# Softplus as one ScalarE function, routing by replaced maxima, and new orders for all engines

## The reference, cut to what matters

```
# state-space block, per sequence
delta = softplus(ts @ dt_w + dt_b)                  # 256 tokens x 256 channels
A = -exp(A_log)                                     # 256 channels x 16 states
dA = exp(A * delta);  new = dA * state + delta * B * h
y = sum over states of (new * C) + D * h;  y * silu(gate), then @ out_w
# feed-forward
probs = softmax(x @ router_w)                       # 8 experts
top_vals, top_idx = top_k(probs, 2);  weights = top_vals / sum(top_vals)
out = sum over e of weight_e * ((x @ w_up[e]) * silu(x @ w_gate[e])) @ w_down[e]
```

## Time and profile before

| | |
|---|---|
| runs | 628.21 us median of 3 (626.58 to 628.58) |
| profiled execution | span 623.0 us (from the first to the last instruction; no other time of it is on record) |
| TensorE busy | 592.8 us, 95% |
| VectorE busy | 499.4 us, 80% |
| ScalarE busy | 400.5 us, 64% |
| GpSimd busy | 392.6 us, 63% |
| mean granted clock of TensorE | 0.989 of 2.4 GHz |

### The profile page before, as it was taken

The page is one execution under the profiler, slowest core; times in us unless marked ns, Lnnn a source line. Parts: engine busy times, 40 slices in busy tenths (PEclk is TensorE's granted clock), DMA queues, the critical chain, the costliest instruction groups (busy, mean ns, idle before and its releaser), DMA issues.

```text
span 623.0 us, 13130 instructions
## 1 busy us (share of the span) xinstructions
PE 592.8 (95%) x4502; PEld 546.7 (88%) x4502; DVE 499.4 (80%) x1094; ACT 400.5 (64%) x897; POOL 392.6 (63%) x368
## 2 busy tenths in 40 slices
PE   6778999699999999999999999999999999999997
PEld 5434786398989999999999999999999999999997
DVE  6798778886998799988998899889988896454454
ACT  7977727766768775878587867776576643516240
POOL 1486564589686987788787978697867773001000
PEclk9779999999999999999999999999999999999999
DMA  7952204130030403021302203030303000000000
GB/s 280 275 169 110 82 2 147 59 119 34 9 140 16 142 4 149 11 89 62 127 23 90 71 12 138 23 136 3 149 12 146 1 15 12 12 2 14 2 22 10
DMA packets 18468, 45.45 MB, mean 73 GB/s; under 512 B 2847, under 2 KB 13664, under 8 KB 14178
## 3 DMA queue, kind: packets, MB, share of 16 engines
q1 hardware_dynamic: 18402, 44.61, 20.1%
HBM read 40.15 MB, written 1.31 MB: 67 GB/s over the span
## 4 chain that ended last, share of the span: by engine, by line
PE 75%; POOL 6%; DVE 5%; issue 3%; ACT 2%; DVEq 0%; POOLq 0%; ACTq 0%
PE ps L1327 25%; PE ps L1131 13%; PE ps L1132 12%; PE ps L1133 12%; PE ps L1376 2%; POOL st L530 2%; DVE st L1005 2%; POOL yacc L543 2%; PE ps L1223 1%; PE ps L1388 1%; PE ps L1295 1%; DVE ps L991 1%; PE ps L1126 1%; PE ps L1367 1%; PE ps L1266 1%
## 5 line engine op out<-in xcount | busy, mean ns | idle before, releaser
L530 POOL TENSOR_TENSOR st<-st,rows_ring 128x512 f32<-128x512 f32 x128 | 165.7, 1298 | 58.5 <-DVE st L1005 58.2
L1327 PE MATMUL ps<-down,inner_ring 128*128 128x128 f32 (+1 forms) x1408 | 171.5, 274 | 0.0
L1327 PEld LDWEIGHTS ps<-down,inner_ring 128*128 128x128 f32 (+1 forms) x1408 | 165.5, 191 | 1.7 <-issue 1.0
L787 ACT ACTIVATE sg<-ps 128x512 f32<-128x512 f32 x176 | 104.3, 596 | 88.1 <-PE ps L1133 76.9
L1080 DVE TENSOR_TENSOR inner_ring<-sg,ps 128x512 f32<-128x512 f32 x176 | 118.7, 678 | 48.6 <-PE ps L1133 25.2
L1005 DVE TENSOR_TENSOR_SCAN st<-dA,ps 128x512 f32<-128x512 f32 x128 | 154.6, 1211 | 2.8 <-ACT dA L730 1.6
L543 POOL TENSOR_TENSOR yacc<-yacc,st 128x512 f32<-128x512 f32 x96 | 123.8, 1289 | 4.8
L730 ACT ACTIVATE dA<-delta,A 128x255 f32<-128x255 f32 x256 | 105.6, 494 | 3.1 <-POOL delta L522 2.8
L1131 PE MATMUL ps<-xhi,up_hi 128*128 128x256 f32 x352 | 104.5, 297 | 1.2 <-DVE inner_ring L1080 0.8
L1133 PE MATMUL ps<-xhi,up_lo 128*128 128x256 f32 x352 | 99.5, 283 | 0.0
L1132 PE MATMUL ps<-xlo,up_hi 128*128 128x256 f32 x352 | 99.4, 283 | 0.0
(11 more groups left out here) (160 smaller groups left out, 923.0 us busy)
## 6 DMA issues: line engine op xcount, KB each, us to landing
rows_ring<-bc SPq DMA_DIRECT2D x31, 1024.0 KB, 4.9
moved_rows<-inner_ring SPq DMA_DIRECT2D x96, 32.0 KB, 1.8
inner_ring<-gate_w SPq DMA_DIRECT2D x1, 1408.0 KB, 7.1
inner_ring<-up_w SPq DMA_DIRECT2D x1, 1408.0 KB, 9.7
down<-down_w SPq DMA_DIRECT2D x2, 512.0 KB, 10.7
out<-X SPq DMA_DIRECT2D x8, 128.0 KB, 1.8
rows_ring<-bc SPq DMA_DIRECT2D x1, 768.0 KB, 5.3
X<-x SPq DMA_DIRECT2D x1, 768.0 KB, 7.5
```

The source lines that it names most:

```text
L530: nc.gpsimd.tensor_tensor(st[:, i % NST], st[:, i % NST], row, ALU.mult).then_inc(s["m_p"], 1)
L787: nc.scalar.activation(sg[:, k % 2], two(bank_of(q, 2 * j)), ACT.Silu).then_inc(s["f_sg"], 1)
L1327: ins = nc.tensor.matmul(bank_of(q, 2 * NP + e)[:, c * H:(c + 1) * H], act_in, down[0:rows, e, n, :], start=n == 0, stop=n == NB - 1)
```

## The change

Softplus is one instruction from PSUM into one of two buffers of `delta`. The logits are summed into SBUF, in rows of 14 whose last six are a large number (BIG); `max` then gives six times BIG and the two largest logits, and `match_replace` writes -BIG where one of these eight stood. What is -BIG afterwards is a chosen expert. The weights of all eight experts come from one tanh each, (1 + tanh(2 l_half - l1_half - l2_half)) / 2 with logits that are halved through the router weights, and GpSimd keeps the chosen ones.

```diff
             def m_delta(u):
+                table("softplus")
                 act.wait_ge(s["m_dt"], u + 1)
+                if u > 1:
+                    act.wait_ge(s["m_dA"], (u - 1) * NS)
+                    act.wait_ge(s["m_dx"], u - 1)
+                nc.scalar.activation(delta[:, u % 2], two(mamba(u)), ACT.Softplus).then_inc(s["m_delta"], 1)
-            def m_abs(u):
-            def m_e(u):
-            def m_u(u):
-            def m_ln(u):
...
-            def m_v(u):
-            def m_pos(u):
...
-                nc.vector.tensor_tensor(delta[:], sp_e[:], sp_p[:], ALU.subtract).then_inc(s["m_delta"], 1)
...
-                nc.gpsimd.tensor_tensor(delta[:], sp_e[:], sp_p[:], ALU.subtract).then_inc(s["m_delta"], 1)
...
-            tables = {"exp": "natural_log_exp_and_others", "silu": "silu_and_others"}
+            tables = {"exp": "exp_and_others", "silu": "silu_and_others", "softplus": "softplus"}
             def r_th(q):
...
+                for c in range(NC):
+                    ins = nc.scalar.activation(w_all[:, c], logit[:, c, 0:NE], ACT.Tanh, bias=r_bias[:, c:c + 1], scale=2.0)
...
+                nc.scalar.activation(w_all[:], w_all[:], ACT.Copy, bias=0.5, scale=0.5).then_inc(s["r_w2"], 1)
-            def r_w2(q):
...
-            def r_index(q):
...
-            def r_spread(q):
...
             def r_top(q):
...
+                nc.vector.tensor_reduce(logit[:, :, 0:NE], parts, AX.X, ALU.add).then_inc(s["r_sum"], 1)
+                dve.wait_ge(s["r_sum"], q + 1)
+                for c in range(NC):
+                    mark(nc.vector.max(top8[:, c, :], logit[:, c, :]))
+            def r_pick(q):
+                link()
+                nc.vector.scalar_tensor_tensor(out=r_bias[:], in0=top8[:, :, NBIG], scalar=-1.0, in1=top8[:, :, NBIG + 1],
+                                               op0=ALU.mult, op1=ALU.subtract).then_inc(s["r_nh"], 1)
...
+                for c in range(NC):
+                    nc.vector.match_replace(picked[:, c, :], top8[:, c, :], logit[:, c, :], -BIG).then_inc(s["r_mr"], 1)
             def r_weight(q):
...
+                nc.gpsimd.tensor_scalar(wts[:, q % 2], picked[:, :, 0:NE], -BIG, None, ALU.is_equal).then_inc(s["r_is"], 1)
...
+                nc.gpsimd.tensor_tensor(wts[:, q % 2], wts[:, q % 2], w_all[:], ALU.mult).then_inc(s["r_w"], 1)
-                reader["chain"] = ("r_dd", NC * (q + 1))
+                reader["chain"] = ("r_sum", q + 1)
-                reader[bank_name(u)] = ("m_pos", u + 1)
+                reader[bank_name(u)] = ("m_delta", u + 1)
```

More of the change, by code:

```diff
@@ L38 @@
 NARROW = 1
+NBIG = 6
+BIG = 3.0e38
 ROWS = P
@@ L62 @@
 """.split()
[L65 to L68, removed]
+AT = {"second": 34.787, "norm": -4.82, "norm2": -0.37, "route": 0.686, "pair": 1.678, "down": 19.361, "expert": 1.546,
+      "attend_norm": 1.007, "attend": 9.632, "attend_stretch": 1.402, "in": -145.221, "in_stretch": 1.739, "soft":
+      -118.544, "early": -85.861, "early_step": 1.169, "late": -50.777, "late_step": 1.679, "scan": -77.2, "state":
+      4.2, "rows": 13.951, "dx": -4.146, "y0": -22.134, "m_out": -2.033, "m_gate": 2.903, "weights": -127.202}
@@ L76 @@
[L76 to L90, removed]
@@ L106 @@
-PACE = {
-        "first": [0.09, -1.89, -0.33, -3.42, -1.1, -1.97, -5.13, -0.29, -0.14, -3.22, -1.72, -1.3, -3.3, -6.2, -5.04, -6.0],
-        "second": [0.44, 1.68, -0.83, -0.46, 1.7, 3.02, 1.89, 4.17, 2.32, 0.61, 0.06, -1.8, -1.74, -3.04, -2.46, -3.54],
-        "third": [1.45, -0.64, 0.18, -1.46, -1.12, 0.13, 1.36, -0.55, 0.02, 5.01, 3.62, 3.69, 1.51, 0.52, -0.75, -2.24],
-        "later": [0.9, 0.39, 1.13, 3.45, 1.49, -0.04, -0.86, 0.72, 0.74, -0.86, 0.42, 0.11, 0.52, -1.24, -0.61, -0.92]}
@@ L111 @@
-LEAD = {"dbx": -7.25, "scan": -8.95}
-STATE = {"dbx": -2.07, "scan": -0.33, "mulC": 1.37, "sum": 4.4}
+M_IN = {"m_stats": -4.023, "m_pow": -0.32, "m_nb": 0.02, "m_norm": 1.573, "m_turn": 1.979, "m_hi": 2.981, "m_lo": 3.9,
+        "m_ph": 4.405, "m_pad": 5.332, "m_tap0": 6.667, "m_cv": 10.746, "m_mul1": 5.474, "m_add1": 6.873, "m_mul2":
+        8.929, "m_add2": 9.004, "m_mul3": 9.14, "m_add3": 9.285, "m_h": 11.512, "m_xp": 13.128, "m_xe": 15.757,
+        "bc_out": 23.604, "m_dt": 17.827, "m_bias": 4.447}
@@ new lines @@
+PAIR = {"gate": -0.262, "up": 1.039, "silu": 0.915, "inner": 1.99}
+EXPERT = {"down": 1.126, "combine": 5.618}
+EARLY = {"f1": [-5.075, -0.551, -0.025, 0.675], "f2": [0.204, 0.253, 0.407, 0.433, 0.295, 0.466, 0.992, 3.191],
+         "scan": [6.802, -2.966, -1.706, -0.844], "state": [-0.093, 0.013, -0.008], "in": [-12.205, 6.283, -5.205,
+         -1.111], "soft": [-12.204, 0.938, -0.02, 1.95], "early": [12.78, -0.915, -5.787, -0.276], "late": [-25.122,
+         0.613, 0.296, -0.485], "attend": [0.642, -1.768, -0.489, -1.421, -0.2, 0.564, 1.311, 2.928]}
@@ new lines @@
+PACE = {"first": [3.026, 4.816, 1.762, 2.657, 0.154, -1.572, -5.203, -5.726, 1.494, -2.015, 2.878, -0.307, -2.8,
+        -4.327, -7.477, -6.722], "second": [-0.868, 1.036, -0.936, -0.724, 1.609, 0.952, 3.873, 1.78, -0.577, -2.6,
+        -4.063, -5.843, -8.223, 1.256, 2.404, 0.48], "third": [1.903, 0.616, 6.6, 7.719, 5.581, 4.473, 3.207, 3.712,
+        1.556, 5.321, 3.764, 2.328, 2.741, 0.64, -0.063, -0.64], "later": [1.321, -0.262, 3.051, 2.666, 1.319, -0.136,
+        -2.0, -3.622, -2.207, -3.023, -1.547, -1.409, -1.507, -0.237, -0.707, -0.854]}
@@ L115, in start_of @@
+LEAD = {"dbx": -4.865, "scan": -2.315}
+STATE = {"dbx": -2.158, "scan": -0.34, "mulC": 1.077, "sum": 4.471}
 def start_of(s, which):
@@ L342, in emptied @@
             return s["f_in" if k % 2 else "f_sg"], q * NP + k // 2 + 1
-        def each(a):
-            return a.unsqueeze(3).broadcast_to([P, NC, 2, NE])
         def run_schedule(share):
@@ L729, in decay @@
                 for it in range(IT):
-                    ins = nc.scalar.activation(dA[:, i % NDA, it, 1:], delta[:, it, 1:], ACT.Exp, scale=A[:, it, n:n + 1])
+                    ins = nc.scalar.activation(dA[:, i % NDA, it, 1:], delta[:, u % 2, it, 1:], ACT.Exp, scale=A[:, it, n:n + 1])
                 ins.then_inc(s["m_dA"], 1)
```

169 lines of the change are left out of this document (58 added, 111 removed).

## The result

The changed kernel takes 616.97 us (median of four runs, 614.07 to 619.37) beside 627.39 us for the kernel before on the same chip: a ratio of 0.985, 95% interval 0.982 to 0.988. The ratio makes 9.4 us less, the difference of the two medians 10.4. The forecast was 621.4 us, the range 614.8 to 626.8. The profiled run took 618.93 us with a span of 617.1 us, so that 1.8 us lie around the span; in every run on record it is 1.7 to 2.0 us.

A forecast was written before the change was run, and what follows sets the result against it. VectorE was taken to set the opening, TensorE's own work plus small stalls the time from q 1. Gains 5.4 + 1.0 + 0.9 - 0.5 = 6.8 us gave span 616.2, time 621.4 us; range 614.8 to 626.8.

The forecast's parts named there:

- Softplus, routing, loads: ScalarE and VectorE: Softplus 0.60 us, replacement 0.16 us, 40 table loads; ScalarE's 4.7 us gain worth nothing by itself.
- First scan at 20.4 us: Opening: the first scan, at 21.79 us before, comes at about 20.4 us, 1.4 us gained.
- The 16 states, 1.6 us shorter: Scan 0 to its last scan's end: 50.4 us instead of 53.39, 3.0 us gained, 1.4 of it the first step's.
- The end of scan 0, gate at 52.9 us, residual at 56.1: Gate of sequence 0 goes first on VectorE; residual at 56.1 us instead of 59.75, 3.6 us gained so far, 1.8 at worst.
- q 0 keeps its length, scan 1 gains 1.8 us: q 0 on TensorE only moves by 3.6 us; the rest of scan 1 takes 26.0 us instead of 27.8.
- q 1 5.4 us earlier: Feed-forward of sequence 1 on TensorE starts 5.4 us earlier, after the gains up to the end of scan 1.
- Behind it 1.9 us less: After q 1's start: 1.0 us from softplus work up to 200 us, 0.9 us from small stalls.
- 0.5 us lost at q 4, 6, 8 and 10: Load and Softplus (1.88 us) between the norm's halves on ScalarE, against 1.6 to 2.1 us of slack: 0.5 us lost.
- What lies around the span, 5.2 us: Median before less its profiled span, 5.2 us, taken as fixed: span 616.2 us gives time 621.4 us.
- The small stalls go too: Stalls from 124 us shrink by over half and the opening's clock stays 2.4 GHz: 614 to 617 us, chance 0.17.
- The opening is GpSimd's: GpSimd's products and splits pace the opening's scans; only 2 to 4 us gained, 624 to 627 us, chance 0.17.
- Slower: Load and Softplus delay the norm at q 2, 4, 6, 8 and 10, costing TensorE 9.4 us: 634.6 us, chance 0.08.

The follow-up runs named there:

- run 1: Both code edits (Softplus, routing by replacement) with every planner order of the kernel before; 624.46 us, ratio 0.9975 to the kernel before.
- run 7: The changed kernel's new orders and new routing, but softplus by its four steps of before and one buffer of delta; 631.27 us, ratio 1.0059 to the kernel before.
- Run 12: The changed kernel with product and scan of state 5 of sequence 1 put back behind inner products 9 and 10 of q 0; 619.73 us.
- run 3: Both code edits, new orders up to the first gate projection of q 1, orders of the kernel before for the rest; 619.47 us, ratio 0.9894.
- run 8: The changed kernel with two more table loads ahead of each Softplus of sequences 2 to 7; 631.07 us, ratio 1.0075 to the kernel before.

## Why the prediction was right, and where it was not

The sign and the range hold, but two of the terms were wrong in opposite directions, and their sum came out by luck. The median lies below the 618 to 624.5 us of the forecast itself. By the forecast's own steps, with the two profiles of the changed kernel:

- **Softplus, routing, loads.** Right in kind: 0.60 us, 0.16 us, 40 loads. "By itself worth nothing" was 1.5 us for both edits (run 1). The Trainium skill (ScalarE: Activation LUTs, What ACT_TABLE_LOAD costs) adds a drain of 1380 ns to each switch; here the next function starts 1.30 us after a load begins (222.39 and 223.69), and three loads in a row take 3.86 us, so the trace disagrees.
- **First scan at 20.4 us: failed.** 22.84 and 21.52 us, and between 21.25 and 23.56 us in ten other profiles, with old and new opening alike (run 7's is later still). What set it in the profile was the first rows of B, for which the product waited 0.90 and 1.99 us. I had added up three queues and taken their common end. In the first profile they are fed by a convolution at half speed. But in the second, where it ran at full speed, the rows were issued at 16.68 us and the product that needs them starts at 20.72, 4.0 us later. For a first scan at 20.4 us, with 0.8 us for the product and 3.8 for the rows, they would have had to be issued at about 15.8 us: their issue is what I had too early.
- **The 16 states, 1.6 us shorter: right.** 31.6 us became 29.8 and, in the second profile, 28.9.
- **The end of scan 0, gate at 52.9 us, residual at 56.1: failed**, and this is the step where the account broke. I let the gate wait for the last product and its sum, 2.4 us. It waits 4.96 us, since the sum stands at the end of a queue of projections, fillers and earlier sums that is late itself. I had counted VectorE and GpSimd through this stretch and of TensorE, busy 30.0 of 36 us before, only that one sum. I had also read the gate's old place, 57.77 us, as VectorE's doing, though TensorE's last sum ended at 57.25. The forecast gained 3.6 us by here; the profiles show 1.2 us lost and 1.1 us gained. The slow product of delta and h (2.51 us in the earlier trace rows) did go: all eight take 0.69 us.
- **q 0 keeps its length, scan 1 gains 1.8 us: too small by 2.9.** From residual to residual were 61.3 us and are 56.6 in both profiles. I had cost this as VectorE's time, with a stall of 2.4 us for sum (1,6). The waits of all scans for TensorE's sums come to 1.2 us in three places. Before, TensorE stood waiting for GpSimd's products in the second half of scan 1; after, it has no idle time there until the gate, and its first sum of scan 1 (1.9 us with the product that opens it) is done before q 0 begins. Of the 4.7 us, 3.3 are idle time of TensorE (5.9 us of it between the residuals before, 2.7 after), and 1.4 are work of TensorE that no longer lies between them. Run 12 shows that it is not the early scan 5 that carries it, and runs 1 and 3 that 0.9 us are the edits' (61.32 to 60.46) and 3.8 the new opening's order. Which of its other moves does, I did not try.
- **q 1 5.4 us earlier.** 3.5 and 5.75 us (120.67 and 118.44 for 124.19): the two errors nearly cancel.
- **Behind it 1.9 us less: 2.4 us.** 498.8 to 496.4 us, and 3.1 us against the edits with the old orders. TensorE's waits there fell from 4.3 to 2.4 us; which order gives which part was not taken apart.
- **0.5 us lost at q 4, 6, 8 and 10: nothing lost**, for another reason than slack. The load and Softplus fill a wait that ScalarE has anyway, for GpSimd's reciprocal root: 0.28 us of it is still left behind them at q 4.
- **What lies around the span, 5.2 us: failed.** I took the median of before less its profiled span for it. In every run it is 1.7 to 2.0 us; the profiled run of before was simply a fast one (623.0 and 1.8 make 624.8, where the median is 627.4). Of the 4.4 us by which the changed kernel's median lies below 621.4, this makes 3.4; with 1.8 us the forecast would have read 618.0, which is the median of all ten runs.
- **The rivals.** 616.97 us lies in the range of "The small stalls go too", but neither of its conditions held: from 124 us on TensorE's idle time fell from 8.3 to 6.3 us and not to half, and the clock of the second stretch was 0.83. "The opening is GpSimd's" was wrong for the changed kernel and right for the one without fillers. "Slower" named the right place: run 8 shows what it costs once those 0.28 us and the slack are used up, and it costs more than the waits alone, since the clock falls too. 634.6 us was worked out without that.

The medians differ by more than the profiles, because the profiled run of before was one of its fast ones and the first profiled run of the changed kernel, at 618.93 us, one of its slow ones. Its ten runs spread over 7 us, and the first four held two at 614 to 615 us.

## What to carry to other kernels

- Cost a stretch for every engine in it, also the one that looked idle before: fillers that cost nothing while TensorE waits are on the path once it does not.
- A cheaper instruction may be worth little in the old order and yet be what a better order needs; measure the edits and the orders apart and together before either is thrown away, and look in the profile for who waits when the old instruction is put in the new order.
- Before a wait is put on TensorE's path, price it twice: once for its length, and once for what the clock does behind it.

## What was not expected of the hardware

**One opening, two times.** The same program has 58.67 and 60.91 us at its first residual, and all of it that the rows account for is the places of its half-speed stretches; differences under 3 us between kernels with such an opening need some ten runs, or profiles compared from a common point.

**Small VectorE operations that last until GpSimd is done.** `n_ve` works on 4 elements, takes 170 ns as a rule and up to 1035 ns. VectorE and GpSimd at such a place, with `n_ve` (L978):

```profile
189.21 0.88 DVE L978 TENSOR_SCALAR n_ve<-n_mv 128x4 f32<-128x4 f32 x1
...
188.79 1.27 POOL L524 TENSOR_TENSOR yacc<-yacc,st 128x512 f32<-128x512 f32 x1
```

GpSimd's sum ends at 190.06 us, VectorE's operation at 190.09. All the long ones of `n_ve` and `r_bias` end 0.02 to 0.03 us behind a GpSimd instruction that was under way when they began. By the Trainium skill (SBUF — State Buffer, Who interferes with whom) VectorE and GpSimd share a pair of ports: a VectorE instruction with two inputs in SBUF, or in a mode that uses both ports, contends for it with a GpSimd instruction that reads SBUF, and in such a mode whoever issues first holds it for the whole instruction. The trace agrees for `r_bias`, which has two inputs in SBUF. `n_ve` has one, and no row shows its mode. This is most of the 9 us that VectorE's busy time did not fall: `n_ve` takes 5.0 us more than before, `r_bias` 4.8 where the comparison that it replaces took 3.0, and three other small groups 2.7. That none of it reaches the span is not shown; for it speaks that TensorE does not wait for the norm at any even q up to q 10.
